# A 16-stage transformer kernel on one core: weight quantisation moved into the expert stages, loads, stores, a norm and the ends of four attention stages rearranged

## The chip, the core and the metric

The kernel runs on one NeuronCore of a Trainium2 chip. The metric is the device time of one execution in microseconds (us); lower is better. The core has five engines that each run their own instructions in order and wait for each other by semaphores: TensorE (PE in the profile, its weight loads PEld), VectorE (DVE), ScalarE (ACT), GpSimd (POOL) and SyncE (SP, which here only issues DMAs). A name with a q, such as SPq, is the engine's sequencer, which issues, waits or branches while the engine itself is idle.

## The reference

One activation `x` of 8 batches x 512 tokens x 128 channels, in fp32, goes through sixteen residual steps. Cut to what matters:

```python
x = X
x = x + attn0a(layernorm(x));  x = x + moe0(layernorm(x))     # 8 experts, top 2
x = x + attn0b(layernorm(x));  x = x + moe0(layernorm(x))
x = x + attn1a(layernorm(x));  x = x + moe1(layernorm(x))     # 8 experts, top 1
x = x + attn1b(layernorm(x));  x = x + moe1(layernorm(x))
x = x + attn2a(layernorm(x));  x = x + fp4_ffn2(layernorm(x)) # quantised weights
x = x + attn2b(layernorm(x));  x = x + fp4_ffn2(layernorm(x))
x = x + attn3a(layernorm(x));  x = x + fp4_ffn3(layernorm(x))
x = x + attn3b(layernorm(x));  x = x + fp4_ffn3(layernorm(x))

def fp4_quant_dequant(x):                # blocks of 16 along the last axis
    scale = max(max(|block|) / 6, 1e-12)
    return GRID[searchsorted(MID, |block / scale|)] * sign(block) * scale
def fp4_ffn(x, w_gate, w_up, w_down):    # 128 -> 352 -> 128
    q = fp4_quant_dequant
    h = silu(q(x) @ q(w_gate).T) * (q(x) @ q(w_up).T)
    return q(h) @ q(w_down).T
```

In `moe0` each token's two expert outputs are weighted by their gates, the token's normalised input is added, and the expert sum is itself layer-normalised. In `moe1` the output of the one chosen expert is added. `attn3b` is a mixer whose last part, the bus, adds to every token of a batch a vector that is computed from the batch's mean.

## The kernel before, in words

The activation `X` and its normalised form `XN` live in SBUF for the whole program, 32 tiles of 128 tokens (4 tiles to a batch). The program is a list of stages, each a `Block`: the engines' programs of a stage start together and the stage ends when the last engine is done. Names in the profile begin with the stage: `l0a`, `l0fa`, `l0b`, `l0fb`, `l1a`, `l1fa`, `l1b`, `l1fb`, `l2a`, `l2fa`, `l2b`, `l2fb`, `l3a`, `l3fa`, `l3b`, `l3fb`.

`load_stage` makes the constants on POOL, the largest and last of them `pick_rows` (L291, L295), and issues on SP one DMA for X and then one for each of 47 weights (L229, L233). Its block ends when SP has issued them all and X has landed. `norm_stage` normalises X on DVE and POOL by halves; it is used before `l0a` and before `l3fb`.

`routed_experts_stage` serves l0f (top 2) and l1f (top 1). It norms batch by batch, picks experts on DVE, sorts the tokens by expert with indirect DMAs on POOL (scatter into `rows_in`), runs fixed blocks of 128 rows, and gathers the results back on POOL (`back<-rows_out`). The batches are cut in chunks by `parts`, (2, 4, 2) in every expert stage; a chunk has `4*K*batches + 7` blocks, so 85 for l0f (K=2) and 53 for l1f (K=1). For a block DVE copies the expert's up weights (`fetch_up`, L3066), PE does the up product (L2817), ACT the Gelu (L2876, L2879) and PE the down product (L2832). While a chunk runs, POOL gathers the one before and scatters the one after, paced by the count of up products. `combine(b)` on DVE (L3037 to L3058) weights, normalises and adds what was gathered for a batch; in l0f ACT takes a square root for it in between (L2867), which DVE waits for and then refines by four small operations. `combine_at` says after which group of blocks a batch is combined. The batches of the last chunk, and those whose turn would come too late, are combined after all blocks.

`heads_attention_stage` serves l0b, l2a, l2b and l3a. A step T is one pair of heads: PE makes the transposed scores (L719) in the PSUM tile `ps_t`, ACT takes the exponential (L827), POOL masks it in the causal stages (L904), and PE multiplies with the values (L766) every second step. 3L steps ahead (L is 8 in l0b and 6 in the others) PE makes the scores once more in `ps_s`, for DVE to take the row maxima (L984). The next scores may only be written when the last exponential has been read out of `ps_t`:

```python
pe.wait_ge(probs_ready.sem, probs_ready.upto(T))
```

`quantized_weights_stage` (names `l2fa_w`, `l3fa_w`) runs before l2fa and before l3fa: DVE quantises `l2f_in` (88 partitions x 1024) and `l2f_out` (128 x 352) in ten operations each (L3150 to L3162), PE transposes them (L3206, L3209) and DVE copies them out of PSUM (L3196, L3198). `quantized_ffn_stage` reads the result. `bus_stage` ends `l3b`: three products (L2562 to L2567), then a scaling (L2578) and one addition over all of X (L2581). `store_stage` writes all of X with one DMA.

## Time and profile before

| what | value |
|---|---|
| median of 3 runs | 4066.81 us (4059.17 to 4073.92) |
| the profiled execution: time, span | 4060.57 us, 4058.8 us |
| TensorE clock granted, mean | 0.833 |
| busy: PE, DVE, ACT, POOL | 2890.8, 2672.3, 1814.9, 1708.3 us |
| load stage until the first instruction of the norm | 30.1 us |
| l0fa, l0fb | 291.5, 293.8 us |
| l1fa, l1fb | 206.1, 206.0 us |
| l0b, l2a, l2b, l3a | 513.4, 404.2, 411.9, 401.6 us |
| quantised weights: l2fa_w, l3fa_w | 16.7, 16.7 us |
| bus, norm before l3fb | 12.1, 23.5 us |

The span runs from the first to the last instruction; the execution's time has 1.8 us more. The stage times are from the first to the last instruction of the stage's names; between stages lie some 0.3 to 3 us. No engine is busy throughout, and the stages follow each other, so what an edit is worth has to be read in its own stage.

### The profile page before, as it was taken

What the parts mean: (1) busy time and instruction counts of PE and PEld (TensorE: products, weight loads), DVE (VectorE), ACT (ScalarE), POOL (GpSimd) and SP (SyncE); (2) the same over time, 40 slices, a digit from 0 to 9 for tenths busy, and PEclk for the clock granted to TensorE, in tenths of its full rate; (3) what the DMA queues carried; (4) which work ended last, traced back from release to release, by engine and by line L of the source; (5) the groups of instructions that cost most, each with busy time, mean ns of one, the idle gap of its engine ahead of it and who ended that gap; (6) DMA issues with size and microseconds to landing.
All of it is one profiled execution on the core that took longest, in us unless ns stands there. A gap on an engine that the chain in (4) does not pass through costs nothing. (4 is left out here: it accounts for less than half of the span.)

```text
span 4058.8 us, 65303 instructions
## 1 busy us (share of the span) xinstructions
PE 2890.8 (71%) x22525; PEld 1821.6 (45%) x22525; DVE 2672.3 (66%) x5940; ACT 1814.9 (45%) x3242; POOL 1708.3 (42%) x2364
## 2 busy tenths in 40 slices
PE   4868467775685759769588847688766888577846
PEld 3768312221684449558333325233344333254534
DVE  4644578884545853353588859688677888495767
ACT  2423247675322324434256634466543466444623
POOL 6743522220535113323456433355444455345753
PEclk9979679997687859869699968699877899786967
DMA  6122232210222012002222100222000221000000
GB/s 184 44 65 87 54 101 85 85 59 1 97 78 62 0 57 71 27 17 77 71 76 80 49 1 1 80 80 73 26 0 32 81 80 65 1 0 1 1 1 21
DMA packets 224583, 209.88 MB, mean 52 GB/s; under 512 B 49687, under 2 KB 201431, under 8 KB 223496
## 3 DMA queue, kind: packets, MB, share of 16 engines
q1 hardware_dynamic: 211976, 180.52, 13.8%
q0 software_dynamic: 12288, 25.19, 2.0%
q8 instruction: 190, 3.11, 0.3%
q14 instruction: 129, 1.06, 0.1%
HBM read 104.86 MB, written 98.83 MB: 50 GB/s over the span
## 5 line engine op out<-in xcount | busy, mean ns | idle before, releaser
L984 DVE TENSOR_REDUCE l0b_negm<-l0b_ps_s 128x2 f32<-128x1024 f32 x256 | 304.2, 1220 | 51.7 <-PE l0b_ps_s L737 50.6
L827 ACT ACTIVATE l0b_E<-l0b_ps_t 128x1024 f32<-128x1024 f32 x256 | 261.8, 1023 | 131.9 <-PE l0b_ps_t L719 131.8
L827 ACT ACTIVATE l2a_E<-l2a_ps_t 128x768 f32<-128x768 f32 (+1 forms) x192 | 169.2, 881 | 130.7 <-PE l2a_ps_t L719 129.9
L827 ACT ACTIVATE l3a_E<-l3a_ps_t 128x768 f32<-128x768 f32 (+1 forms) x192 | 169.2, 881 | 125.5 <-PE l3a_ps_t L719 124.6
L827 ACT ACTIVATE l2b_E<-l2b_ps_t 128x768 f32<-128x768 f32 (+1 forms) x192 | 169.1, 881 | 108.7 <-PE l2b_ps_t L719 107.7
L984 DVE TENSOR_REDUCE l2b_negm<-l2b_ps_s 128x2 f32<-128x256 f32 (+3 forms) x256 | 196.4, 818 | 28.8 <-PE l2b_ps_s L742 28.6
L984 DVE TENSOR_REDUCE l3a_negm<-l3a_ps_s 128x2 f32<-128x256 f32 (+3 forms) x256 | 196.4, 819 | 16.6 <-PE l3a_ps_s L742 16.5
L984 DVE TENSOR_REDUCE l2a_negm<-l2a_ps_s 128x2 f32<-128x256 f32 (+3 forms) x256 | 196.1, 817 | 15.3 <-PE l2a_ps_s L742 15.2
L904 POOL TENSOR_SCALAR_AFFINE_SELECT l2b_E<-l2b_E 128x256 f32<-128x256 f32 x256 | 100.3, 407 | 179.3 <-ACT l2b_E L827 179.3
L904 POOL TENSOR_SCALAR_AFFINE_SELECT l2a_E<-l2a_E 128x256 f32<-128x256 f32 x256 | 101.1, 407 | 167.5 <-ACT l2a_E L827 165.8
L904 POOL TENSOR_SCALAR_AFFINE_SELECT l3a_E<-l3a_E 128x256 f32<-128x256 f32 x256 | 101.1, 407 | 163.8 <-ACT l3a_E L827 162.2
L719 PE MATMUL l0b_ps_t<-room_up,room_down 51*128 51x512 bf16 x512 | 104.1, 403 | 82.7 <-ACT l0b_E L827 73.1
L766 PE MATMUL l0b_ps_v<-l0b_E,l0b_v 128*32 128x512 f32 x1024 | 144.9, 640 | 0.0
L719 PEld LDWEIGHTS l0b_ps_t<-room_up,room_down 51*128 51x128 bf16 x512 | 24.8, 93 | 229.6 <-ACT l0b_E L827 218.5
L2832 PE MATMUL l0fb_ps_y<-room_down,l0fb_hT 128*128 x680 | 97.8, 291 | 22.4 <-ACT l0fb_hT L2876 22.4
L2876 ACT ACTIVATE l0fb_hT<-l0fb_ps_u 128x512 f32<-128x512 f32 x85 | 50.3, 597 | 141.0 <-PE l0fb_ps_u L2817 141.0
L2876 ACT ACTIVATE l0fa_hT<-l0fa_ps_u 128x512 f32<-128x512 f32 x85 | 50.3, 597 | 138.5 <-PE l0fa_ps_u L2817 138.4
L2832 PE MATMUL l0fa_ps_y<-room_down,l0fa_hT 128*128 x680 | 96.1, 287 | 22.5 <-ACT l0fa_hT L2876 22.5
L737 PE MATMUL l0b_ps_s<-room_down,room_up 48*128 48x512 bf16 x512 | 86.8, 400 | 24.7 <-DVE l0b_negm L984 20.9
L719 PE MATMUL l2b_ps_t<-room_up,room_down 51*128 51x256 bf16 (+3 forms) x512 | 71.0, 316 | 44.2 <-ACT l2b_E L827 40.7
L2832 PEld LDWEIGHTS l0fb_ps_y<-room_down,l0fb_hT 128*128 128x128 f32 x680 | 90.2, 207 | 23.2 <-issue 23.2
L2817 PE MATMUL l0fb_ps_u<-l0fb_xT,l0fb_own_up 128*128 128x128 f32 x680 | 96.1, 288 | 4.7 <-DVE l0fb_xT L3020 4.7
(970 smaller groups left out, 8793.3 us busy)
## 6 DMA issues: line engine op xcount, KB each, us to landing
room_up<-l0b_stack SPq DMA_DIRECT2D x32, 192.0 KB
room_down<-l0b_stack SPq DMA_DIRECT2D x32, 192.0 KB
room_up<-l2a_stack SPq DMA_DIRECT2D x32, 192.0 KB
room_down<-l2a_stack SPq DMA_DIRECT2D x32, 192.0 KB
room_up<-l2b_stack SPq DMA_DIRECT2D x32, 192.0 KB
room_down<-l2b_stack SPq DMA_DIRECT2D x32, 192.0 KB
room_up<-l3a_stack SPq DMA_DIRECT2D x32, 192.0 KB
room_down<-l3a_stack SPq DMA_DIRECT2D x32, 192.0 KB
```

The costliest lines, as they stand in the source:

```text
L719: mm = pe.matmul(ps_t[:, hh, off:off + n], ks[b % 2][r, j, kt * P:(kt + 1) * P], qs[b % 2][r, j, first_q[kt]:S], start=True, stop=True)
L737: mm = pe.matmul(ps[:, hh, off:off + keys[qt]], qs[b % 2][r, j, qt * P:(qt + 1) * P], ks[b % 2][r, j, 0:keys[qt]], start=True, stop=not ca ...
L766: mm = pe.matmul(ps_v[32 * a:32 * a + 32, first_q[kt]:S], v_row[b % 2][:, kt, col:col + 32], e[:, a, off:off + w_k], start=(kt == 0), stop ...
L827: act.activation(probs(n % 3, c, 0)[:, 2 * p:2 * p + 2, :], ps_t[:, :, 0:width[c]], ACT.Exp, scale=scale).then_inc(probs_ready.sem, 1)
L904: kept = pool.affine_select(out=here, in_=here, compare_op=ALU.is_ge, fill=0.0, base=0, pattern=[[0, 2], [1, P]], channel_multiplier=-1)
L984: e = dve.tensor_reduce(negm[:, qt, :, j], ps_s[n % 2][:, :, off:off + keys[qt]], AX.X, ALU.max, negate=True)
L2817: mm = pe.matmul(ps_u[j % 4][:, c, :], own_up[j % 3][:, c * P:(c + 1) * P], xT[G % 2][:, k, :], start=True, stop=True)
L2832: mm = pe.matmul(ps_y[G % 2][:, k, :], hT[j % 3][:, c, :], down[:, bass.ds(e, 1), c, :].rearrange("p a b -> p (a b)"), start=(b2 is None a ...
L2876: a = act.activation(hT[j % 3][:, :, :], ps_u[j % 4][:, :, :], ACT.Gelu)
```

## The change

- **Loads.** `load_stage` issues X, `l0a_w` and `l0a_masks` only, and waits for these three. The other 45 weights are issued by SP inside the first `norm_stage`; SP waits for them at the end of the `l0a` stage. `pick_rows` is made by POOL at the end of that norm stage.
- **Stores.** `store_stage` is gone. SP stores each batch inside the last feed-forward stage.
- **Bus.** The scaling, the addition and the norm before l3fb are one loop over batches in the bus stage: DVE scales and adds, takes the statistics and shifts, POOL the roots, ACT normalises. The norm stage is gone.
- **Quantised weights.** The two stages are gone. The twenty DVE operations stand one by one in the block loop of l1fa (for layer 2) and l1fb (for layer 3), at blocks 8 to 27; PE transposes after the last block, DVE copies the result over the weights' own tiles.
- **Expert stages.** A batch is combined in steps: weighting at block START, statistics at START+1, rescaling and adding at START+3. The root is a `pow` on POOL; the four refining operations and ACT's square root are gone. POOL takes the roots of the late batches after its last gather. l1f has parts (4, 4) in place of (2, 4, 2): 46 blocks; l0f keeps (2, 4, 2).
- **Attention ends.** From step ALL-3L+2 on, when `ps_s` is no longer needed, the transposed scores go round `ps_t`, `ps_s[0]`, `ps_s[1]`, and PE waits for the exponential of three steps before.

```diff
+FIRST = ("l0a_w", "l0a_masks")
+def load_weight(core, sp, name):
+    src = core.dram[name]
+    return sp.dma_start(core.w[name][tuple(slice(0, x) for x in src.shape)], src)
...
-            for name, src in dram_now.items():
-                if name != "X":
-                    dst = core.w[name][tuple(slice(0, x) for x in src.shape)]
-                    sp.dma_start(dst, src).then_inc(core.loads, 16)
-            sp.wait_ge(done, 16)
+            for name in FIRST:
+                load_weight(core, sp, name).then_inc(done, 16)
+            sp.wait_ge(done, 16 * (1 + len(FIRST)))
...
         if core.loads_pending:
             @block.sync
             def _(sp):
-                sp.wait_ge(core.loads, pending)
+                for weight in core.dram:
+                    if weight != "X" and weight not in FIRST and weight not in LATER:
+                        load_weight(core, sp, weight).then_inc(core.loads, 16)
...
-                pe.wait_ge(probs_ready.sem, probs_ready.upto(T))
+                if T <= LAST:
+                    pe.wait_ge(probs_ready.sem, probs_ready.upto(T))
+                elif T <= LAST + 2:
+                    pe.wait_ge(scores_read.sem, scores_read.upto(ALL))
+                else:
+                    pe.wait_ge(probs_ready.sem, probs_ready.upto(T - 2))
...
-                        mm = pe.matmul(ps_t[:, hh, off:off + n], ks[b % 2][r, j, kt * P:(kt + 1) * P],
+                        mm = pe.matmul(scores_room(T)[:, hh, off:off + n], ks[b % 2][r, j, kt * P:(kt + 1) * P],
...
-            dve.tensor_scalar(y[:, :, :], ps_y[:, :, :], 0.1, None, ALU.mult).then_inc(copied, 1)
+            for b in range(B + 1):
+                if b < B:
+                    xb = core.X[:, b * TB:(b + 1) * TB, :]
+                    ch.link(dve.scalar_tensor_tensor(xb, ps_y[:, b, :].rearrange("p (a d) -> p a d", a=1).broadcast_to([P, TB, D]), 0.1, xb,
+                                                     ALU.mult, ALU.add))
+                    rows.statistics(dve, ch, b)
+                if b >= 1:
+                    rows.shifts(dve, b - 1)
...
+            def combine_roots(b):
+                pool.wait_ge(stats_ready.sem, stats_ready.upto(b + 1))
+                pool.tensor_tensor(rstd[:, b % 2, :], var[:, b % 2, :], core.minus_half[:, 0:TB], ALU.pow).then_inc(roots_ready.sem, 1)
...
             for t, k in moves(CHUNKS - 1):
                 gather_row(t, k)
+            for b in range(B):
+                if top2 and START[b] == LAST:
+                    combine_roots(b)
...
+            for j in range(LAST):
+                G = group_of[j]
+                if j == begin[G] and G + 1 < ALL:
                     read_xT(G + 1)
+                if j + 3 < LAST:
+                    fetch_up(j + 3)
+                if j + 1 == end[G]:
+                    read_y(G)
+                    if top2 and G < B:
+                        add_normed(G)
+                for b in range(B):
+                    if START[b] < LAST and 0 <= j - START[b] <= FINISH:
+                        combine_step(b, j - START[b])
+                if coming is not None and QUANTISE <= j < QUANTISE + 20:
+                    quantise_step(j - QUANTISE)
+            if coming is not None:
+                read_coming()
+            late = [b for b in range(B) if START[b] == LAST]
+            for b in late:
+                weigh(b)
+                if top2:
+                    moments(b)
+                    if b - 1 in late:
+                        add_scaled(b - 1)
+            if top2:
+                add_scaled(late[-1])
...
-    routed_experts_stage(core, name, w["l1f_gate"], w["l1f_bias"], w["l1f_up"], w["l1f_down"], b1=w["l1f_b1"], b2=w["l1f_b2"], parts=(2, 4, 2))
+    routed_experts_stage(core, name, w["l1f_gate"], w["l1f_bias"], w["l1f_up"], w["l1f_down"], b1=w["l1f_b1"], b2=w["l1f_b2"], parts=(4, 4),
+                         coming="l2f" if first else "l3f")
...
+                for b in range(B):
+                    sp.wait_ge(out_read.sem, out_read.upto(2 * (b + 1)))
+                    tiles = slice(b * TB, (b + 1) * TB)
+                    sp.dma_start(token_view(out)[:, tiles, :], core.X[:, tiles, :]).then_inc(stored, 16)
```

START of a batch is computed from the pace of the gathers. For l0f it is block 36, 44, 72 and 77 for batches 0 to 3, and batches 4 to 7 are late; for l1f it is 32, 36 and 40 for batches 0 to 2, and batches 3 to 7 are late.

## Rows read from the trace of the kernel before

**Rows 1.** The page, busy time of the engines in the whole span.

```profile
PE 2890.8 (71%) x22525; PEld 1821.6 (45%) x22525; DVE 2672.3 (66%) x5940; ACT 1814.9 (45%) x3242; POOL 1708.3 (42%) x2364
```

**Rows 2.** The DMAs of 0 to 12 us: issue, size, us to landing.

```profile
X<-in_X SPq DMA_DIRECT2D x1, 0.5 KB, 10.1
```

**Rows 3.** Timelines of 0 to 60 us: start, duration, engine, line, what.

```profile
9.44 3.38 POOL L295 TENSOR_SCALAR_AFFINE_SELECT pick_rows<-pick_rows 32x1024 bf16<-32x1024 bf16 x3
...
29.15 0.43 SPq L233 DMA_DIRECT2D l3b_bus<-in_l3b_bus  x1
...
30.08 0.87 DVE L348 BATCH_NORM_STATS2 l0a_norm_stats<-X 128x6 f32<-128x128 f32 x4 [30.08 <-PEq L226]
...
52.05 1.64 POOL L337 TENSOR_SCALAR XN<-X,l0a_norm_mv,l0a_norm_rstd 128x128 f32<-128x128 f32 x2
55.34 8.61 SPq L1551 DMA_DIRECT2D rows_in<-zeros  x2
```

**Rows 4.** The DMAs of 4040 to 4060 us and of 1630 to 1660 us.

```profile
out<-X SPq DMA_DIRECT2D x1, 2048.0 KB, 8.7
...
rows_out<-l1fa_y SPq DMA_DIRECT2D x2, 256.0 KB, 2.3
```

**Rows 5.** Timeline of the bus and the norm behind it.

```profile
3869.73 1.22 DVE L2578 TENSOR_SCALAR l3b_bus_y<-l3b_bus_ps_y 128x1024 f32<-128x1024 f32 x1 [3.66 <-PE l3b_bus_ps_y L2567]
...
3899.53 0.69 DVE L3305 TENSOR_REDUCE l3fb_x_scale<-XN 128x32 f32<-128x512 f32 x1 [1.41 <-PEq L313]
```

**Rows 6.** Timeline of the second weight stage and the start of l3fa.

```profile
3506.25 1.22 DVE L3150 TENSOR_REDUCE l3fa_w_scale<-l3f_in 88x64 f32<-88x1024 f32 x1 [2.00 <-PEq L497]
...
3509.79 0.69 DVE L3158 TENSOR_SCALAR l3fa_w_power<-l3fa_w_v 88x1024 uint32<-88x1024 uint32 x1
...
3523.28 0.69 DVE L3305 TENSOR_REDUCE l3fa_x_scale<-XN 128x32 f32<-128x512 f32 x1 [0.30 <-PEq L3170]
```

**Rows 7.** Instructions by line, l0fa, 300 to 450 us: busy, mean ns, idle before.

```profile
L2832 PE MATMUL l0fa_ps_y<-room_down,l0fa_hT 128*128 x504 | 72.0, 289 | 22.5 <-ACT l0fa_hT L2876 22.5
```

**Rows 8.** Timeline of the end of l0fa.

```profile
454.36 0.94 POOL L2733 DMA_INDIRECT l0fa_back<-rows_out,l0fa_slot_u  x1 [9.02 <-DMA rows_out<-l0fa_y]
...
473.62 0.94 POOL L2733 DMA_INDIRECT l0fa_back<-rows_out,l0fa_slot_u  x1 [0.30 <-issue]
476.08 0.88 DVE L3037 TENSOR_SCALAR l0fa_back<-l0fa_back,l0fa_gate 128x128 f32<-128x128 f32 x4 [3.86 <-DMA l0fa_back<-rows_out,l0fa_slot_u]
...
479.48 0.17 DVE L3049 TENSOR_SCALAR l0fa_var<-l0fa_mv 128x4 f32<-128x4 f32 x1
...
480.73 1.12 DVE L3056 TENSOR_SCALAR l0fa_back<-l0fa_back,l0fa_mv,l0fa_rstd 128x128 f32<-128x128 f32 x4
481.88 0.69 DVE L3058 TENSOR_TENSOR X<-X,l0fa_back 128x512 f32<-128x512 f32 x1
```

**Rows 9.** Timelines of l1fa: the first scatter, the third and the last Gelu.

```profile
1486.47 1.09 POOL L2729 DMA_INDIRECT rows_in<-XN,l1fa_slot_u  x1 [0.18 <-issue]
...
1524.80 1.14 ACT L2879 ACTIVATE l1fa_hT<-l1fa_ps_u,l1fa_b_block 128x128 f32<-128x128 f32 x4 [4.25 <-PE l1fa_ps_u L2817]
...
1649.46 1.14 ACT L2879 ACTIVATE l1fa_hT<-l1fa_ps_u,l1fa_b_block 128x128 f32<-128x128 f32 x4 [1.25 <-PE l1fa_ps_u L2817]
```

**Rows 10.** Busy time by engine in a stretch of l1fa's blocks.

```profile
1560.00:1600.00 40.00, 40.00 (x305) 36.14 (x305) 13.68 (x26) 18.18 (x65) 15.89 (x16) 1.00 0.26 77
```

**Rows 11.** Instructions by line, last 22 steps of l0b, 944 to 987.5 us.

```profile
L827 ACT ACTIVATE l0b_E<-l0b_ps_t 128x1024 f32<-128x1024 f32 x22 | 22.5, 1023 | 18.1 <-PE l0b_ps_t L719 18.1
L766 PE MATMUL l0b_ps_v<-l0b_E,l0b_v 128*32 128x512 f32 x88 | 18.7, 937 | 0.0
```

**Rows 12.** Busy time and granted clock in a stretch of these steps.

```profile
960.00:970.00 10.00, 7.76 (x34) 1.78 (x38) 1.21 (x5) 4.20 (x5) 1.26 (x1) 0.50 0.00 0
```

**Rows 13.** Instructions by line, last 14 steps of l2a, and of l3a.

```profile
L827 ACT ACTIVATE l2a_E<-l2a_ps_t 128x768 f32<-128x768 f32 (+1 forms) x14 | 12.2, 870 | 9.7 <-PE l2a_ps_t L719 9.7
...
L827 ACT ACTIVATE l3a_E<-l3a_ps_t 128x768 f32<-128x768 f32 (+1 forms) x14 | 12.2, 871 | 7.9 <-PE l3a_ps_t L719 7.7
```

More of the change, by code:

```diff
@@ L368, in _ @@
                 normalise(pool, b, (2, 3)).then_inc(pool_norm_ready.sem, 1)
+            if core.loads_pending:
+                pick = core.pick_rows
+                pool.memset(pick[:, :, :], 0.0).then_inc(core.picks_made, 1)
+                pool.wait_ge(core.picks_made, 1)
+                for k in range(3):
+                    r = slice(32 * k, 32 * k + 32)
+                    pool.affine_select(out=pick[r, :, :], in_=pick[r, :, :], compare_op=ALU.not_equal, fill=1.0, base=0,
+                                       pattern=[[-1, B], [0, P]], channel_multiplier=1).then_inc(core.picks_made, 1)
+                pool.wait_ge(core.picks_made, 4)
         if turned:
@@ L2577, in _, with routed_experts_stage @@
             dve.wait_ge(in_psum, 3)
-            dve.tensor_scalar(y[:, :, :], ps_y[:, :, :], 0.1, None, ALU.mult).then_inc(copied, 1)
-            dve.wait_ge(copied, 3)
-            x = core.X[:, :, :].rearrange("p (b t) d -> p b t d", b=B)
-            dve.tensor_tensor(x, x, y[:, :, :].rearrange("p b (a d) -> p b a d", a=1).broadcast_to([P, B, TB, D]),
-                              ALU.add).then_inc(copied, 1)
-def routed_experts_stage(core, name, w, bias, up, down, top2=False, b1=None, b2=None, parts=(4, 4)):
+            ch = Chain(dve_step, dve, 0)
+            for b in range(B + 1):
[6 more added lines that the diff above has]
+                    rows.shifts(dve, b - 1)
+            dve_step.per = ch.k
+        @block.gpsimd
+        def _(pool):
+            for b in range(B):
+                rows.roots(pool, b)
+        @block.scalar
+        def _(act):
+            for b in range(B):
+                rows.normalise(act, b)
+    core.end(1, [dve_step])
+    for unused in (rows.T_in_psum, rows.T_ready):
+        unused.per = 0
+    rows.end()
+def routed_experts_stage(core, name, w, bias, up, down, top2=False, b1=None, b2=None, parts=(4, 4), coming=None):
     nc = core.nc
@@ L2863, in _ @@
                 expert_exponentials(1)
-            def roots(b):
-                act.wait_ge(stats_ready.sem, stats_ready.upto(b + 1))
-                act.activation(rstd[:, :], var[:, :], ACT.Sqrt).then_inc(roots_ready.sem, 1)
             for j in range(LAST):
@@ L2881, in _ @@
                 a.then_inc(act_ready.sem, 1)
-                if top2 and j + 1 == end[group_of[j]]:
-                    for b in combine_at(group_of[j]):
-                        roots(b)
-            if top2:
-                for b in combine_at(ALL):
-                    roots(b)
         @block.vector
@@ L3092, in routed_experts_stage @@
     stats_ready.per = roots_ready.per = B * top2
+    quant_ready.per = quantT_in_psum.per = int(coming is not None)
     core.end(1, sig)
@@ L3260, in blocks, with _ @@
             return x.rearrange("p t (n c) -> p (t n) c", c=BLOCK)
+        if out is not None:
+            stored = core.ctx.enter_context(nc.semaphore("stored"))
+            @block.sync
+            def _(sp):
+                for b in range(B):
+                    sp.wait_ge(out_read.sem, out_read.upto(2 * (b + 1)))
+                    tiles = slice(b * TB, (b + 1) * TB)
+                    sp.dma_start(token_view(out)[:, tiles, :], core.X[:, tiles, :]).then_inc(stored, 16)
+                sp.wait_ge(stored, 16 * B)
         def x_tiles(u):
@@ L3494, in attention_program @@
             stage(core)
-        store_stage(core, out)
 def layer0_attention_a(core):
```

273 lines of the change are left out of this document (134 added, 139 removed).

## The prediction

> **What bounds the kernel now.** I read the page first. No engine is near full: PE is busy for 71% of the span, DVE for 66% [rows 1], and the chain that ended last reaches back only into the last feed-forward stage. The stages run one after another, so I looked up where each begins and ends, and then, at the places that the diff touches, the timelines, the instructions by line and the windows. What the reader is to see is a set of stretches in which most engines wait for one thing: SP's issues at the start, DVE alone on the weights, POOL's gathers behind the expert blocks, one PSUM tile at the ends of the attentions. The change goes at eight such stretches, and the sum is theirs. It is made against the profiled execution (4060.6 us, its span and 1.8 us around it), which lies 6.2 us under the median of 4066.8; the saving is then taken from the median.
>
> **Loads: minus 16.** The norm starts at 30.08, when SP has issued its last weight at 29.15 to 29.58 [rows 3], though X had landed 10.1 us after its issue at 0.85, at 11.0 [rows 2]. Behind X only two small loads are left, so the norm should start at about 11 (10 to 12): 19 saved. Given back: POOL makes `pick_rows` behind its last normalisation, which ends at 53.7; the three selects take 3.38 and the memset about 1, so the stage, which gave way at 55.3, ends some 3 us later relative to its start [rows 3]. SP's 45 issues at 0.47 us (one of many such in a row; the last is in [rows 3]) take 21 to 22 us and stay under the stage's 28. If they took as long as the whole load stage, 28 us, they would still be level with POOL. The wait for them at the end of l0a, a whole stage on, costs nothing. 16, between 14 and 18.
>
> **Stores: minus 7.** The output's one DMA lands 8.7 us after its issue; 256 KB to HBM land in 2.3 [rows 4]. Seven of eight batches leave during the stage. 6.5, and with the missing stage border 7.
>
> **Bus and norm: minus 9.** From the end of the products to the first instruction of l3fb pass 3899.53 - 3869.73 = 29.8 us [rows 5]. The joint loop costs DVE per batch one scaled add over 512 columns (0.69, as the addition of that size in [rows 8]), statistics, aggregation, variance (1.4 together, four tiles at the 0.87 of [rows 3] and the small ones) and a shift, about 2.15; eight make 17.2. Behind the last come a root (1.0), the shift, ACT's four tiles (1.7) and the border: 3.4. 29.8 - 20.6 = 9, between 7 and 10.
>
> **The two weight stages: minus 34.** The second takes 3523.28 - 3506.25 = 17.0 with its border, the first the same [rows 6]. The work goes into l1f's blocks. Its largest operation is 1.22 us, five of 20 are; the 20 sum to 13. DVE is busy 13.7 of 40 us there and PE 40 of 40 at full clock [rows 10], and the copies of up weights have two blocks of lead, so I cost it at nothing: PE's work is the cover. Without that cover it would cost 13 per stage. The final transposes and copies, about 4, lie in the wait for the last stores and gathers.
> One rule speaks against this. The rows show 0.69 us for each of two big `tensor_scalar` operations on SBUF [rows 6]. The Trainium skill, "SBUF — State Buffer", section "SBUF: two separate sides", says that while DVE is in a two-port mode GpSimd can't write the descriptors of its DMAs. By that rule the four such operations of a stage would hold back POOL's scatters by at most 2 us in all; by the rows POOL is busy 15.9 of 40 us and idle in front of each paced DMA [rows 10], which takes it up. Either way the sum stays.
>
> **l1f in two chunks: minus 13 for both.** The third to the last Gelu of 53 take 1649.46 - 1524.80 = 124.7 for 50 blocks, 2.49 each [rows 9]; seven blocks fewer save 17.5. The last chunk has four batches, so 8 more gathers at 1.25 us (the pace of [rows 8]) stand behind the last store: 10 given back. In front, the first route waits for four batches, and 16 rather than 8 tiles are scattered before the first fetch: the first scatter moves from 1486.5 to about 1490, and 16 at 1.26 end near 1510, with landing, fetch and transpose 1516. Before, DVE's routing of the other chunks let the first product start only near 1515, so only 1 to 2 are lost. Net 6 to 7 per stage, 13 for both (between 6 and 18).
>
> **l0f: minus 34 for both.** Between 300 and 450 us PE is idle for 22.5 us in front of the down product, waiting for a Gelu [rows 7]: ACT stands in the square root of a combine, behind DVE, four times in the stage. Some 5 us more go in products at half clock after these waits. Spread over four blocks, with the root on POOL, this goes, except where POOL, which in the last chunk issues DMAs without a gap, comes late with batches 2 and 3: I give back 3. So the blocks end about 24 us earlier. At the end the change is dearer. Today DVE combines as the data come and is done at 482.57, 8.0 us after the last gather's end at 474.56 [rows 8]. After, the root of batch 4 stands behind all 16 gathers, and everything that follows on DVE waits for it: root 1.1; then in order rescale(4) 1.8, weigh and statistics(6) 3.6, rescale(5) 1.8, weigh and statistics(7) 3.6, rescale(6) 1.8, rescale(7) 1.8. The 3.6 is 476.08 to 479.65, the 1.8 is 480.73 to 482.57 [rows 8]. That makes 15.6 in place of 8.0: 7.5 given back. 24 - 7 = 17 per stage, 34 for both, between 16 and 42.
>
> **Attention ends: minus 27.** In l0b's last 22 steps ACT's exponentials take 22.5 us and wait 18.1 us for PE's scores [rows 11], because PE may write them only after the exponential before. With three tiles PE runs ahead. If it is at full clock, nearly all of the 18 goes, 16. It is at the lower level of 1.2 GHz there now and busy 78% [rows 12]: if that stays, the 43.5 us hold 34 us of PE work, and 9.5 go. The value products are the dearest, 937 ns for one of four that overlap [rows 11]. Full clock is likelier, since less waiting leaves PE busier; I take 12. In the last 14 steps of l2a the waits are 9.7, in l3a 7.9, and l2b is as l3a [rows 13]; a read of the group's output and POOL's masks leave 3 to 4 of them: 6 + 4.5 + 4.5 = 15. Together 27, between 17 and 38.
>
> **Sum.** 16 + 7 + 9 + 34 + 13 + 34 + 27 = 140. The profiled execution would be near 3921, the median 4066.8 - 140 = 3927; the three runs of before lie between 4059 and 4074, so I round to 3925.
>
> **Rivals.** (a) The l0f tail eats more and PE stays at 1.2 GHz at the attention ends: l0f 8 per stage, ends 17 together, 140 - 18 - 10 = 112 saved, 3955. For it: the clock of [rows 12]. Against: that clock is seen while PE waits.
> (b) The added DVE steps are not hidden in l1f: 2 x 13 for the operations and 2 x 4 for the transposes and copies, 140 - 34 = 106, 3961. Against it: [rows 10].
> (c) All goes by the better bounds: loads 18, stores 7, bus 10, weights 34, l1f 16, l0f 42, ends 38: 165, 3902. For it: PE is idle only where it waits for what is removed.
> (d) Slower than before. The DVE steps thin PE's stream in l1f so far that the lower clock level is granted for the blocks. PE is full there at the higher level [rows 10], so a block would cost up to 2.4 more, and the 92 blocks of both stages 220: 4147. It decides once 58 of the 92 blocks run at the low level. Against it: PE has two blocks of lead over DVE.
>
> **How the numbers follow.** Chances: my sum 0.70, (a) 0.12, (b) 0.05, (c) 0.11, (d) 0.02. 3925 is the likeliest case. The range 3895 to 3968 takes in (a), (b) and (c) with the scatter of the runs (some 7 us either way) and leaves out (d) and the far ends of the parts. A change within 0.3% (12 us) is what a measurement of this kernel can't tell from none; all cases but (d) are far past it, so faster 0.97, same 0.01, slower 0.02.
>
> **What would show it.** The norm starting at about 11 us and l0a at about 39; no names of weight stages or of the last norm; the first operation of l3fb some 21 us after the bus products; a last DMA of 2 to 3 us. In l0fa no Sqrt on ACT and next to no idle PE in front of the down products, but the last DVE instruction 15 to 16 us behind the last gather. In l1fa 46 blocks still 2.5 apart, with DVE near half busy, and the last gather 20 us after the first of its batch. In l0b's last 22 steps exponentials 1.05 to 1.5 us apart. The prediction would be wrong if blocks 8 to 27 of l1f are longer than the others, if POOL's roots hold DVE in the middle of l0f, or if the granted clock of the attention ends stays 0.5 and their steps as long as now.

## The result, and the profile after

| what | before | after |
|---|---|---|
| median of 4 runs each | 4066.1 us (4059.2 to 4073.9) | 3919.3 us (3917.5 to 3924.9) |
| ratio, 95% interval | | 0.9641 (0.9621 to 0.9661) |
| the profiled execution: time, span | 4060.6, 4058.8 us | 3924.9, 3923.1 us |
| TensorE clock granted, mean | 0.833 | 0.842 |

The change saves 146.8 us by the medians and 135.7 us by the two profiled executions; 140 was predicted, and 3925 for the median, 3921 for the profiled execution. The first line of the page, the answer to [rows 1]:

```profile
PE 2817.3 (72%) x22261; PEld 1768.3 (45%) x22261; DVE 2638.8 (67%) x5824; ACT 1783.6 (45%) x3184; POOL 1713.8 (44%) x2364
```

Where the 135.7 us came from, as stage to stage distances (first instruction of a stage to the first of the next) of the two traces:

| term | predicted | measured | what it is made of |
|---|---|---|---|
| loads | 16 | 14.1 | norm starts 17.4 earlier, its stage is 3.3 longer |
| stores | 7 | 7.9 | l3fb with the store 159.3 to 151.4 |
| bus and norm | 9 | 8.6 | 36.2 to 27.6 |
| two weight stages | 34 | 34.1 | 17.0 each |
| l1f in two chunks, with the quantise steps | 13 | 15.2 | 7.5 and 7.7 |
| l0f | 34 | 25.1 | 11.8 and 13.3 |
| attention ends | 27 | 30.7 | l0b 17.5, l2a 5.2, l2b 3.1, l3a 4.9 |
| the rest | 0 | 0.0 | l3fa 1.9 shorter, mixer 3.0 longer, and others |

**The start.** DMAs of 0 to 14 us (issue, size, us to landing), the answer to [rows 2]:

```profile
l0a_masks<-in_l0a_masks SPq DMA_DIRECT2D x1, 66.5 KB, 4.9
...
X<-in_X SPq DMA_DIRECT2D x1, 0.5 KB, 10.0
```

and the timeline of 0 to 43 us, the answer to [rows 3]:

```profile
0.85 0.91 SPq L238 DMA_DIRECT2D X<-in_X  x1
...
1.81 5.48 SPq L173 DMA_DIRECT2D l0a_w<-in_l0a_w  x1
...
7.33 0.43 SPq L173 DMA_DIRECT2D l0a_masks<-in_l0a_masks  x1
...
12.68 0.87 DVE L338 BATCH_NORM_STATS2 l0a_norm_stats<-X 128x6 f32<-128x128 f32 x4 [12.68 <-PEq L235]
...
36.27 0.95 POOL L361 MEMSET pick_rows<- 96x1024 bf16 x1
37.37 3.38 POOL L365 TENSOR_SCALAR_AFFINE_SELECT pick_rows<-pick_rows 32x1024 bf16<-32x1024 bf16 x3
41.21 1.89 POOL L1612 MEMSET l0a_v<- 128x2144 f32 x1 [0.46 <-POOLq L303]
```

X lands at 10.9, but the norm starts at 12.7: SP is held for 5.5 us by its second issue, so `l0a_masks` is issued only at 7.3 and lands at 12.2. The 45 later loads don't show: `pick_rows` closes the stage. The kernel before has the same hold at its second issue, of another weight, and its trace could have told of it:

```profile
1.80 5.40 SPq L233 DMA_DIRECT2D rope<-in_rope  x1
```

**Stores and bus.** The last output DMAs (answer to [rows 4]), and the timeline from the end of the bus products to l3fb (answer to [rows 5]):

```profile
out<-X SPq DMA_DIRECT2D x3, 256.0 KB, 2.3
```

```profile
3750.66 0.69 DVE L2594 SCALAR_TENSOR_TENSOR X<-l3b_bus_ps_y,X 128x512 f32<-128x512 f32 x1 [3.84 <-PE l3b_bus_ps_y L2579]
...
3771.71 0.69 DVE L3372 TENSOR_REDUCE l3fb_x_scale<-XN 128x32 f32<-128x512 f32 x1 [2.31 <-PEq L2557]
```

21.05 us in place of 29.8.

**l1fa.** A stretch of the blocks that carry the quantise steps, 40 us with busy time by engine (PE, PEld, DVE, ACT, POOL), granted clock, DMA share and GB/s; the answer to [rows 10]:

```profile
1500.00:1540.00 40.00, 40.00 (x305) 36.14 (x305) 20.23 (x40) 18.34 (x66) 8.90 (x10) 1.00 0.24 67
```

DVE has 6.5 us more to do than in [rows 10], PE is still busy throughout and at full clock.

**l0fa.** Its down products between 280 and 412 us (instructions by line), the answer to [rows 7]; the idle time in front of them is gone:

```profile
L2887 PE MATMUL l0fa_ps_y<-room_down,l0fa_hT 128*128 x512 | 69.0, 279 | 0.0
```

The end of the stage, the answer to [rows 8]:

```profile
419.28 0.17 DVE L3155 TENSOR_SCALAR l0fa_var<-l0fa_mv 128x4 f32<-128x4 f32 x1
...
434.12 0.94 POOL L2774 DMA_INDIRECT l0fa_back<-rows_out,l0fa_slot_u  x1 [0.30 <-issue]
435.08 2.02 POOL L2779 TENSOR_TENSOR l0fa_rstd<-l0fa_var,minus_half 128x4 f32<-128x4 f32 x2
...
436.16 1.11 DVE L3161 TENSOR_SCALAR l0fa_back<-l0fa_back,l0fa_mv,l0fa_rstd 128x128 f32<-128x128 f32 x4 [16.71 <-POOL l0fa_rstd L2779]
...
447.04 1.03 POOL L2779 TENSOR_TENSOR l0fa_rstd<-l0fa_var,minus_half 128x4 f32<-128x4 f32 x1 [4.32 <-DVE l0fa_var L3155]
...
449.89 0.69 DVE L3164 TENSOR_TENSOR X<-X,l0fa_back 128x512 f32<-128x512 f32 x1
...
457.60 0.88 DVE L413 BATCH_NORM_STATS2 l0b_row_stats<-X 128x6 f32<-128x128 f32 x4 [7.01 <-PEq L2639]
```

DVE has the variances of batches 4 and 5 at 419.4 and then waits 16.7 us for their roots, which stand behind the gathers; that was foreseen. The last line was not: DVE is done at 450.6, but the next stage starts 7.0 us later. Before, it started 1.5 us after DVE. The engine that closes the stage is POOL. Its sequencer has a record there that the timeline leaves out (start, us):

```
447.01 10.31 POOL sequencer L2639 DRAIN
457.36  0.02 POOL sequencer L2639 EVENT_SEMAPHORE
```

Each stage ends with one on each engine. On POOL most of them end at most 0.3 us after POOL's last instruction; those of the expert stages end 9.2 us after it in l0f and 5.3 us after it in l1f, before the change as after it.

**Attention ends.** Instructions by line in the last 22 steps of l0b, the answer to [rows 11]:

```profile
L836 ACT ACTIVATE l0b_E<-l0b_ps_s 128x1024 f32<-128x1024 f32 x14 | 14.0, 1048 | 1.9 <-PE l0b_ps_s L728 1.9
L775 PE MATMUL l0b_ps_v<-l0b_E,l0b_v 128*32 128x512 f32 x92 | 13.2, 644 | 3.7 <-ACT l0b_E L836 2.1 <-ACT l0b_oT L844 1.6
L836 ACT ACTIVATE l0b_E<-l0b_ps_t 128x1024 f32<-128x1024 f32 x8 | 8.4, 1046 | 0.3 <-PE l0b_ps_t L728 0.3
```

and busy time by engine in two stretches of them, the answer to [rows 12]:

```profile
925.00:935.00 10.00, 8.57 (x66) 1.80 (x64) 2.93 (x13) 9.67 (x11) 0.76 (x1) 1.00 0.00 1
935.00:945.00 10.00, 8.00 (x60) 1.69 (x60) 0.55 (x2) 9.67 (x12) 0.51 (x1) 1.00 0.00 0
```

ACT waits 2.2 us instead of 18.1, and the granted clock in these stretches is 1.00 instead of 0.50 (over the 22 steps 0.93 instead of 0.62). The 22 steps take 24.4 us instead of 43.9. In the last 14 steps of l2a and l3a, the answer to [rows 13], ACT still waits 4.0 and 4.8 us:

```profile
L836 ACT ACTIVATE l2a_E<-l2a_ps_s 128x768 f32<-128x768 f32 (+1 forms) x9 | 8.0, 905 | 4.0 <-PE l2a_ps_s L728 4.0
...
L836 ACT ACTIVATE l3a_E<-l3a_ps_s 128x768 f32<-128x768 f32 (+1 forms) x9 | 8.1, 908 | 4.8 <-PE l3a_ps_s L728 4.8
```

### The profile page after: what moved, and what is told of

Same layout as the page of the kernel before. It is cut to its first block and busy times, and to the rows that moved or that the text cites. A ratio compares the mean times of both kernels' runs of the same rounds, so it can differ in the third digit from the quotient of the medians.

```text
span 3923.1 us, 64375 instructions
## 1 busy us (share of the span) xinstructions
PE 2817.3 (72%) x22261; PEld 1768.3 (45%) x22261; DVE 2638.8 (67%) x5824; ACT 1783.6 (45%) x3184; POOL 1713.8 (44%) x2364
## 3 DMA queue, kind: packets, MB, share of 16 engines
q1 hardware_dynamic: 208376, 178.69, 14.1%
## 5 line engine op out<-in xcount | busy, mean ns | idle before, releaser
L836 ACT ACTIVATE l0b_E<-l0b_ps_t 128x1024 f32<-128x1024 f32 x242 | 247.8, 1024 | 117.6 <-PE l0b_ps_t L728 117.4
L836 ACT ACTIVATE l2a_E<-l2a_ps_t 128x768 f32<-128x768 f32 (+1 forms) x182 | 160.4, 881 | 119.7 <-PE l2a_ps_t L728 118.9
L836 ACT ACTIVATE l3a_E<-l3a_ps_t 128x768 f32<-128x768 f32 (+1 forms) x182 | 160.4, 881 | 117.1 <-PE l3a_ps_t L728 116.3
L993 DVE TENSOR_REDUCE l2a_negm<-l2a_ps_s 128x2 f32<-128x256 f32 (+3 forms) x256 | 195.9, 816 | 14.9 <-PE l2a_ps_s L751 14.8
L836 ACT ACTIVATE l2b_E<-l2b_ps_t 128x768 f32<-128x768 f32 (+1 forms) x182 | 160.3, 881 | 100.3 <-PE l2b_ps_t L728 99.5
L728 PE MATMUL l0b_ps_t<-room_up,room_down 51*128 51x512 bf16 x484 | 96.2, 394 | 70.2 <-ACT l0b_E L836 60.9
L728 PEld LDWEIGHTS l0b_ps_t<-room_up,room_down 51*128 51x128 bf16 x484 | 23.3, 93 | 204.5 <-ACT l0b_E L836 193.8
L746 PE MATMUL l0b_ps_s<-room_down,room_up 48*128 48x512 bf16 x512 | 87.8, 404 | 25.7 <-DVE l0b_negm L993 22.7
L2872 PE MATMUL l0fa_ps_u<-l0fa_xT,l0fa_own_up 128*128 128x128 f32 x680 | 94.1, 283 | 9.3 <-DVE l0fa_xT L3120 4.8
L775 PE MATMUL l2b_ps_v<-l2b_E,l2b_v 128*32 128x512 f32 (+3 forms) x1024 | 93.9, 463 | 8.9 <-POOL l2b_E L913 6.9
L775 PE MATMUL l2a_ps_v<-l2a_E,l2a_v 128*32 128x512 f32 (+3 forms) x1024 | 91.7, 453 | 4.9 <-ACT l2a_oT L844 2.3
L775 PE MATMUL l3a_ps_v<-l3a_E,l3a_v 128*32 128x512 f32 (+3 forms) x1024 | 91.6, 452 | 4.7 <-ACT l3a_oT L844 2.9
## 6 DMA issues: line engine op xcount, KB each, us to landing
room_up<-l0b_stack SPq DMA_DIRECT2D x32, 192.0 KB
room_down<-l0b_stack SPq DMA_DIRECT2D x32, 192.0 KB
room_up<-l2a_stack SPq DMA_DIRECT2D x32, 192.0 KB
room_down<-l2a_stack SPq DMA_DIRECT2D x32, 192.0 KB
room_up<-l2b_stack SPq DMA_DIRECT2D x32, 192.0 KB
room_down<-l2b_stack SPq DMA_DIRECT2D x32, 192.0 KB
room_up<-l3a_stack SPq DMA_DIRECT2D x32, 192.0 KB
room_down<-l3a_stack SPq DMA_DIRECT2D x32, 192.0 KB
```

The lines of the kernel that those rows point to most:

```text
L728: mm = pe.matmul(scores_room(T)[:, hh, off:off + n], ks[b % 2][r, j, kt * P:(kt + 1) * P], qs[b % 2][r, j, first_q[kt]:S], start=True, sto ...
L746: mm = pe.matmul(ps[:, hh, off:off + keys[qt]], qs[b % 2][r, j, qt * P:(qt + 1) * P], ks[b % 2][r, j, 0:keys[qt]], start=True, stop=not ca ...
L775: mm = pe.matmul(ps_v[32 * a:32 * a + 32, first_q[kt]:S], v_row[b % 2][:, kt, col:col + 32], e[:, a, off:off + w_k], start=(kt == 0), stop ...
L836: act.activation(probs(n % 3, c, 0)[:, 2 * p:2 * p + 2, :], scores_room(T)[:, :, 0:width[c]], ACT.Exp, scale=scale).then_inc(probs_ready.s ...
L993: e = dve.tensor_reduce(negm[:, qt, :, j], ps_s[n % 2][:, :, off:off + keys[qt]], AX.X, ALU.max, negate=True)
L2872: mm = pe.matmul(ps_u[j % 4][:, c, :], own_up[j % 3][:, c * P:(c + 1) * P], xT[G % 2][:, k, :], start=True, stop=True)
```

## The experiments

All start from the kernel after. Total times are medians of four runs; the kernel after was 3919.3. An untouched stage can differ by 2 to 7 us from one run to the next (below), so effects of a few us are read in their own stage.

### The late roots on ACT

POOL's part behind its last gather goes, ACT's comes behind its last Gelu; the third hunk is `add_scaled` on DVE.

```diff
-            for b in range(B):
-                if top2 and START[b] == LAST:
-                    combine_roots(b)
...
+            for b in range(B):
+                if top2 and START[b] == LAST:
+                    act.wait_ge(stats_ready.sem, stats_ready.upto(b + 1))
+                    act.activation(rstd[:, b % 2, :], var[:, b % 2, :], ACT.Sqrt).then_inc(roots_ready.sem, 1)
...
+                if START[b] == LAST:
+                    r, v = rstd[:, u, :], var[:, u, :]
+                    ch.link(dve.reciprocal(r, r))
+                    ch.link(dve.scalar_tensor_tensor(corr[:, :], r, -0.5, r, ALU.mult, ALU.mult))
+                    ch.link(dve.tensor_tensor(corr[:, :], corr[:, :], v, ALU.mult))
+                    ch.link(dve.scalar_tensor_tensor(r, corr[:, :], 1.5, r, ALU.add, ALU.mult))
```

> Base: the kernel after. In l0fa and l0fb the four roots of the batches that are combined after all blocks (4 to 7) go from POOL to ACT (a Sqrt, then a reciprocal and three small DVE operations); POOL keeps the roots inside the loop. In the kernel after, POOL's last gather of l0fa ends at 435.1 us, its last root at 448.1, DVE's last addition at 450.6, and the next stage's first instruction starts at 457.6, 7.0 after it, when POOL's sequencer record DRAIN has ended. Theory A (the stage's end is POOL's closing DRAIN, and that ends some 9.3 us after POOL's last instruction, whatever it is): POOL's last instruction is now the last gather, so the border lies at 435.1 + 9.3 = 444.4 or at the end of DVE's additions, whichever is later; DVE no longer waits 16.7 us for roots behind the gathers and ends near 444. 12 to 13 us shorter per stage, 25 in all. Rival B (the border follows DVE's end by 7 us for another reason): DVE's end moves by 6 to 7 us and the border with it, 13 us in all. Rival C (the DRAIN lasts from the last gather, and roots behind it cost nothing): the next stage starts at the same time as now, 0 us in all.

Measured: 3890.0 us, ratio to the kernel before 0.9567 (0.9551 to 0.9583); l0fa 11.0 and l0fb 11.7 us shorter. Timeline of the end of l0fa:

```profile
434.70 0.95 POOL L2775 DMA_INDIRECT l0fa_back<-rows_out,l0fa_slot_u  x1 [0.30 <-issue]
...
445.42 0.69 DVE L3172 TENSOR_TENSOR X<-X,l0fa_back 128x512 f32<-128x512 f32 x1
446.65 0.87 DVE L413 BATCH_NORM_STATS2 l0b_row_stats<-X 128x6 f32<-128x128 f32 x4 [0.54 <-PEq L2639]
```

POOL's DRAIN ends at 444.9, 9.2 us after the last gather, and DVE at 446.1 is last again: the border is 0.5 us. 22.7 us of the 29 stand in these two stages; B asked for 13 and C for none. Theory A holds, less 1 to 2 us because DVE ends 2 us later than I had worked out.

### An explicit drain ahead of the last gathers

```diff
+            pool.drain()
             wait_stored(CHUNKS - 1)
             for t, k in moves(CHUNKS - 1):
                 gather_row(t, k)
```

> Base: the kernel after, with one explicit drain on POOL in each expert stage, ahead of the gathers of the last chunk (112 of l0f's 128 indirect DMAs and 48 of l1f's 64 are then issued). The closing DRAIN ends 9.3 us after POOL's last instruction in l0f and 5.3 us in l1f: 1.3 us plus 0.0625 us for each indirect DMA of the stage fits both. Theory A (the drain pays for each indirect DMA since the drain before): the added drain takes 8.3 us in l0f, where POOL has only 4.5 us to spare (last gathers start 3.8 later), and the closing one 2.3 instead of 9.3, so the stage is about 3 us shorter; in l1f POOL is idle for 22 us there, so the added drain is hidden and the next stage starts 2 to 3 us earlier (DVE's last addition is then last). About 10 us less in all. Rival B (the closing DRAIN is a fixed time after the last DMAs, or is set by the stage): the closing one stays at 9.3 and 5.3 us, l0f gets up to 5 us longer per stage and l1f stays: 0 to 10 us more in all.

Measured: 3904.3 us; l1fa and l1fb 2.7 and 2.5 us shorter, l0fa 0.5 longer, l0fb 2.3 shorter. Timeline of POOL and DVE around the two drains of l0fa and behind the last gather of l1fa:

```profile
411.40 0.94 POOL L2774 DMA_INDIRECT l0fa_back<-rows_out,l0fa_slot_u  x1 [0.30 <-issue]
422.33 0.94 POOL L2774 DMA_INDIRECT l0fa_back<-rows_out,l0fa_slot_u  x1 [9.99 <-issue]
...
456.82 0.69 DVE L3165 TENSOR_TENSOR X<-X,l0fa_back 128x512 f32<-128x512 f32 x1
458.05 0.87 DVE L413 BATCH_NORM_STATS2 l0b_row_stats<-X 128x6 f32<-128x128 f32 x4 [0.54 <-PEq L2639]
...
1595.21 0.87 DVE L413 BATCH_NORM_STATS2 l1b_row_stats<-X 128x6 f32<-128x128 f32 x4 [0.53 <-PEq L2639]
```

The added drain takes 9.2 us in l0fa (412.3 to 421.6, with 112 indirect DMAs issued) and 4.0 in l1fa (48), where it lies in idle time. The closing one ends 1.4 us after POOL's last instruction in l0fa and 2.2 after it in l1fa, at 1592.4 to 1594.6 (16 DMAs each), instead of 9.2 and 5.3. So a drain pays for what was issued since the drain before it, and it can be paid early. Rival B is out. 4.0, 5.3 and 9.2 us for 48, 64 and 112 are 0.08 us each, and 128 take 9.2 as well; my line of 1.3 + 0.0625 gave 8.3 for 112 and was 0.9 too low. The 3 us that theory A expected of an l0f stage did not come in l0fa: POOL's last root ends 7.0 us later there, and DVE, done at 457.5, is last. Why l0fb gained 2.3 all the same is not shown. The stages give 7.1 us together, the medians 15.0 and the two profiled executions 22.0; of the difference in the latter 11.8 us lie in stages that the edit doesn't touch (l0b 5.5, l2a 3.3, mixer 3.0).

### l1f in three chunks again

```diff
-    routed_experts_stage(core, name, w["l1f_gate"], w["l1f_bias"], w["l1f_up"], w["l1f_down"], b1=w["l1f_b1"], b2=w["l1f_b2"], parts=(4, 4),
+    routed_experts_stage(core, name, w["l1f_gate"], w["l1f_bias"], w["l1f_up"], w["l1f_down"], b1=w["l1f_b1"], b2=w["l1f_b2"], parts=(2, 4, 2),
```

> Base: the kernel after, with l1f's experts in three chunks (2, 4, 2) again, 53 blocks instead of 46 in l1fa and in l1fb. The step of the prediction was 13 us for both stages (6 to 18); the stages themselves became 7.5 and 7.7 us shorter. If the two chunks did all of that: 13 to 16 us slower, each l1f stage by 6.5 to 8. Rival (the chunks are worth their blocks in full, at 2.39 us for a block of l1fa and 7 blocks fewer, and the quantise steps took some of it back): 30 us slower, or more.

Measured: 3927.1 us. l1fa is 5.2 and l1fb 8.2 us longer, 13.4 together, as in the prediction's step. The medians show 7.8 of it and the two profiled executions 2.8: in the latter l0b was 7.0 and l2b 3.7 us shorter, with the same code. The rival is out, and its block was wrong: from the third to the last Gelu the blocks of l1fa are 2.49 us apart in both kernels and in this run, not 2.39. Seven of them are 17.5 us, and the last gather ends 23.1 us behind the last down product with two chunks and 13.4 with three, so the prediction's 10 given back are there too and nothing is left to explain. That l1fa lost less than l1fb lies ahead of the blocks: its third Gelu comes 60.5 us into the stage in this run, that of l1fb after 62.3.

### One PSUM tile for the last scores

```diff
-            return (ps_t, ps_s[0], ps_s[1])[(T - LAST) % 3] if T >= LAST else ps_t
+            return ps_t
...
-                if T <= LAST:
-                    pe.wait_ge(probs_ready.sem, probs_ready.upto(T))
-                elif T <= LAST + 2:
-                    pe.wait_ge(scores_read.sem, scores_read.upto(ALL))
-                else:
-                    pe.wait_ge(probs_ready.sem, probs_ready.upto(T - 2))
+                pe.wait_ge(probs_ready.sem, probs_ready.upto(T))
```

> Base: the kernel after, with the last scores of l0b, l2a, l2b and l3a again all in one PSUM tile and each behind the exponential before it. The stages became 17.5, 5.2, 3.2 and 4.9 us shorter. If that is all due to the three tiles: 31 us slower, more than half of it in l0b, with the last exponentials of l0b again 1.5 to 2.4 us apart (they are 0.90 to 0.92 apart now). Rival (part of it came from the stages ahead of them or from the clock): under 25 us slower.

Measured: 3966.5 us, 47 more. Instructions by line in l0b's last 22 steps:

```profile
L831 ACT ACTIVATE l0b_E<-l0b_ps_t 128x1024 f32<-128x1024 f32 x22 | 22.5, 1024 | 19.2 <-PE l0b_ps_t L723 19.2
L770 PE MATMUL l0b_ps_v<-l0b_E,l0b_v 128*32 128x512 f32 x88 | 19.5, 977 | 0.0
```

and all 22 steps by engine (PE first, then PEld, DVE, ACT, POOL), in this run and in the kernel after:

```profile
916.90:961.90 45.00, 32.29 (x146) 6.28 (x146) 3.84 (x16) 24.02 (x26) 1.26 (x1) 0.59 0.00 1
920.80:945.20 24.40, 20.77 (x146) 4.83 (x145) 3.85 (x16) 22.15 (x26) 1.27 (x1) 0.93 0.01 2
```

From the first of the last 22 exponentials (l0b) or 14 (the others) to the end of the last: 45.0, 25.0, 23.6 and 24.0 us with one tile; 24.4, 16.8, 16.0 and 17.5 with three. The difference is 20.6 + 8.2 + 7.6 + 6.5 = 42.9 us, more than either theory. Of l0b's 20.6, ACT's waits are 19.2 - 2.2 = 17, and 2.7 (22 times 0.12) is that exponentials of 1.02 us follow each other every 0.90 us once their input is ready. Seen from TensorE, its idle time falls by 9.1 us (12.7 to 3.6) and the same 146 products take 11.5 us less, at a mean clock of 0.93 instead of 0.59; no run changes the clock alone. The rival falls too: ahead of the ends the four stages differ by at most 1 us each.

The edit does not give back the times of before, though the code of these steps is the same: before they took 43.9, 23.9, 21.4 and 21.4 us, 7.0 less in all, at mean clocks of 0.62, 0.64, 0.84 and 0.84, and here they run at 0.59, 0.56, 0.71 and 0.64. So the change itself brought 35.9 us in these steps, and the other 7.0 of the 42.9 go with the clock that this run happened to get in them.

### No quantise steps in l1f

The twenty operations of each l1f stage are left out, so the weights of layers 2 and 3 are transposed but not quantised.

```diff
-                if coming is not None and QUANTISE <= j < QUANTISE + 20:
-                    quantise_step(j - QUANTISE)
+                if coming is not None and j == QUANTISE + 19:
+                    dve.sem_inc(quant_ready.sem, 1)
```

> Base: the kernel after without the twenty quantise operations in each l1f stage; the weights of layers 2 and 3 are transposed but left unquantised. Theory (they are hidden behind blocks that TensorE bounds at full clock): l1fa and l1fb stay within 1 us each of 201.9 and 201.6 us. Rival (b of the prediction, they sit in DVE's way to the next block): up to 13 us less in each, 26 in all. The 7 blocks fewer should have brought 16.7 us per stage at 2.39 us each and brought 7.6; if the quantise operations took the rest, 9 us less in each.

Measured: 3915.4 us (3911.6 to 3923.7), which overlaps the runs of the kernel after. l1fa takes 201.8 us as before the edit (201.9), l1fb 204.5 instead of 201.6, longer with less work: its clock reached 1.00 in the fifth stretch of 20 us instead of the fourth. The stretch of l1fa's blocks by engine:

```profile
1494.00:1534.00 40.00, 40.00 (x306) 36.14 (x305) 11.95 (x24) 18.34 (x66) 8.78 (x10) 1.00 0.24 67
```

DVE loses 8.3 of its 20.2 us and PE runs on as it did. The steps are hidden in full; rival (b) is out. The transposes and copies, which this run keeps, lie in the 23.1 us between the last down product and the last gather: DVE's last addition of l1fa ends 2.3 us behind the last gather, before the change and after it.

### pick_rows in the load stage

The first hunk is POOL's program in the load stage, the second the one in `norm_stage`.

```diff
+            pool.memset(pick[:, :, :], 0.0).then_inc(core.picks_made, 1)
+            pool.wait_ge(core.picks_made, 1)
+            for k in range(3):
+                r = slice(32 * k, 32 * k + 32)
+                pool.affine_select(out=pick[r, :, :], in_=pick[r, :, :], compare_op=ALU.not_equal, fill=1.0, base=0,
+                                   pattern=[[-1, B], [0, P]], channel_multiplier=1).then_inc(core.picks_made, 1)
             pool.wait_ge(made, 33)
+            pool.wait_ge(core.picks_made, 4)
...
-            if core.loads_pending:
-                pick = core.pick_rows
-                pool.memset(pick[:, :, :], 0.0).then_inc(core.picks_made, 1)
...
-                pool.wait_ge(core.picks_made, 4)
```

> Base: the kernel after, with the memset and the three selects of pick_rows again at the end of POOL's work in the load stage. There the stage already waits until 12.2 us for the last of its three transfers, and POOL's part (5.5 us for these four, from the 36.3 to 40.8 us that they take now and a memset) would end near 13. Theory: the norm starts about 0.5 us later and the norm's stage is 3.2 us shorter (28.5 to 25.3), 2.5 to 3 us less in all. Rival: POOL's work in the load stage ends later than that and the load stage gives all of it back: 0.

Measured: 3911.2 us. Timeline:

```profile
9.43 3.38 POOL L302 TENSOR_SCALAR_AFFINE_SELECT pick_rows<-pick_rows 32x1024 bf16<-32x1024 bf16 x3
...
13.37 0.87 DVE L346 BATCH_NORM_STATS2 l0a_norm_stats<-X 128x6 f32<-128x128 f32 x4 [13.37 <-PEq L235]
```

The norm starts 0.7 us later, its stage is 3.3 us shorter, and l0a starts at 38.6 instead of 41.2: 2.6 us, as expected. The other 5 us of the total are not the edit's.

### All roots on ACT

On top of the late roots on ACT; the lines stand behind the Gelu of block j, and the four refining operations now follow every root. POOL takes none: its list `rooted_within` is empty.

```diff
+                for b in range(B):
+                    if top2 and START[b] < LAST and j == START[b] + FINISH - 1:
+                        act.wait_ge(stats_ready.sem, stats_ready.upto(b + 1))
+                        act.activation(rstd[:, b % 2, :], var[:, b % 2, :], ACT.Sqrt).then_inc(roots_ready.sem, 1)
```

> Base: the kernel roots_on_act; now the four roots inside the block loop are ACT's too, each behind the Gelu of the block in which POOL took it, with a reciprocal and three small DVE operations behind it. The split of a batch's combining over four blocks stays. Compared are l0fa and l0fb (270.2 and 270.1 us in roots_on_act). Theory A (the loop's gain of 24.5 us per stage came from ACT no longer waiting between two Gelus for a root's input, and from no change of ACT's function tables): with the input ready two blocks before, only the changes of table are left, twice 1 to 1.3 us for each of four roots, 5 to 10 us more per stage. Rival B (it was the split over four blocks alone): the stages stay within 2 us. Rival C (ACT's queue is the bound, any root in it stalls the Gelu for good): 20 to 25 us more per stage, as before.

Measured: 3905.0 us; l0fa 280.0 and l0fb 279.9 us, 9.8 more each than with the loop's roots on POOL. ACT, and the down products, between 300 and 407 us, by line:

```profile
L2941 ACT ACT_TABLE_LOAD x4 | 5.1, 1283 | 0.1
L2932 ACT ACT_TABLE_LOAD x3 | 3.8, 1283 | 0.1
L2941 ACT ACTIVATE l0fa_rstd<-l0fa_var 128x4 f32<-128x4 f32 x3 | 0.6, 205 | 5.4 <-DVE l0fa_var L3161 5.4
...
L2885 PE MATMUL l0fa_ps_y<-room_down,l0fa_hT 128*128 x400 | 54.0, 279 | 6.7 <-ACT l0fa_hT L2932 6.7
```

Timeline of ACT around one of these roots:

```profile
335.88 1.28 ACT L2941 ACT_TABLE_LOAD   x1
339.10 0.21 ACT L2941 ACTIVATE l0fa_rstd<-l0fa_var 128x4 f32<-128x4 f32 x1 [1.93 <-DVE l0fa_var L3161]
339.32 1.28 ACT L2932 ACT_TABLE_LOAD   x1
340.61 1.09 ACT L2932 ACTIVATE l0fa_hT<-l0fa_ps_u 128x512 f32<-128x512 f32 x2
```

The size is that of theory A, at its upper end: 9.8 / 4 = 2.45 us for each root in the loop. Its reason holds in part. The two table loads of 1.28 us are there, but the input is not ready: ACT waits another 1.6 to 2.5 us for the variances at each of the four roots (5.0 at each before the change). A root holds ACT for 4.4 to 5.3 us between two Gelus, and how the 2.45 us that reach the blocks divide between loads and wait is not shown. B and C are out. The Trainium skill, "ScalarE: Activation LUTs", section "What ACT_TABLE_LOAD costs", gives 1.28 us for the load and 2.66 for a whole switch. The load agrees with this trace, the whole switch does not: from the end of the Sqrt to the start of the next Gelu pass 1.30 us (339.31 to 340.61). An estimate from the page's larger figure, two switches for each of four roots, would be 21 us of ACT. The blocks end 245.2 us into the stage here, 260.0 before the change and 235.4 after it. So 14.8 of the 24.5 us came from splitting the combining over four blocks and 9.8 from taking the root away from ACT, with its loads, the wait that was left and the refining operations.

### Combined

The late roots on ACT, `pick_rows` in the load stage, and the explicit drain in l1f alone.

```diff
+            if not top2:
+                pool.drain()
             wait_stored(CHUNKS - 1)
```

> Base: the kernel roots_on_act (3890.0 us), with pick_rows made in the load stage and with POOL's explicit drain ahead of the last gathers in the l1f stages alone, where POOL is idle for 22 us. Theory: 3 us less from the first, 2.5 to 2.8 us less in each of the two l1f stages as in drain_early, so 8 to 8.5 less: 3881 to 3882 us. Rival (the gains don't add, the clock takes them back): 3885 us or more.

Measured: 3881.0 us (3875.9 to 3883.7), ratio to the kernel before 0.9555 (0.9539 to 0.9571). The l1f stages are 2.9 us shorter each, l0a starts 2.6 us earlier, l0f as with the roots on ACT. The gains add up.

### Combined, with one more drain and another order at l0f's end

```diff
+                if top2 and c == 1:
+                    pool.drain()
                 wait_stored(c - 1)
...
             for b in late:
+                awaited = b >= first_batch[CHUNKS - 1]
+                if top2 and awaited:
+                    add_scaled(b - 1)
                 weigh(b)
                 if top2:
                     moments(b)
-                    if b - 1 in late:
+                    if not awaited and b - 1 in late:
                         add_scaled(b - 1)
```

> Base: the kernel combined (3881.0 us), where DVE's last addition of l0fa ends at 441.2 us and the next stage starts at 441.8. Two edits in l0f: one more explicit drain on POOL, ahead of its wait for the first chunk's stored rows, where POOL is idle for 15 us in l0fa; and on DVE the scaling and addition of the batch before goes ahead of the wait for the gathers of batches 6 and 7 instead of behind their moments. Theory (the closing DRAIN pays for what was issued since the last drain, now 80 indirect DMAs instead of 128, some 6.5 us instead of 9.2 after the last gather; DVE has one scaling and addition less, 1.7 to 2.7 us, behind the last gather): the next stage starts 1.5 to 2.5 us earlier, 3 to 5 us less in all, 3876 to 3878 us. Rival (the closing DRAIN does not get shorter by a drain that far back): it ends 9.2 us after the last gather, which is 1.3 us before the start of the next stage now, so at most 1.3 us less per stage.

Measured: 3880.3 us (3878.9 to 3887.6), ratio 0.9538 (0.9519 to 0.9557); l0fa 1.6 and l0fb 2.1 us shorter. Timeline of the end of l0fa:

```profile
430.71 0.94 POOL L2774 DMA_INDIRECT l0fa_back<-rows_out,l0fa_slot_u  x1 [0.30 <-issue]
...
439.08 0.69 DVE L3175 TENSOR_TENSOR X<-X,l0fa_back 128x512 f32<-128x512 f32 x1
440.31 0.87 DVE L412 BATCH_NORM_STATS2 l0b_row_stats<-X 128x6 f32<-128x128 f32 x4 [0.54 <-PEq L2638]
```

The closing DRAIN ends at 438.2, 6.6 us after the last gather, for 80 DMAs: 6.5 was expected. The stages show the 3.7 us; the total can't be told from the kernel combined, because l2fa, l2fb, l2b and the mixer took 1.6 to 2.9 us more each.

## Why the prediction was right

The total was right (3919 against 3925, inside the range) because the mechanisms and most of the terms were. That it came so close is in part luck: against 140 the two profiled executions give 135.7, in which l0f is 8.9 and the loads 1.9 short, and the attention ends 3.7 and l1f 2.2 over; and the medians differ by 11 us more than the profiled executions.

- **Loads, 14.1 for 16.** The step "behind X only two small loads are left, so the norm should start at about 11" failed by 0.7 us against its own upper bound of 12: the issue of the second load held SP for 5.5 us, and l0a starts at 41.2 instead of about 39. The 3 us for `pick_rows` were right, and `picks_in_load` gets 2.6 back.
- **Stores 7.9, bus 8.6, weights 34.1** for 7, 9 and 34. The bus loop has a period of 2.19 us for 2.15. That the steps are covered is shown by `no_quantise`.
- **l1f, 15.2 for 13**, and 13.4 when undone alone. 17.5 saved and 10 given back were right to 0.1 us in l1fa. The 1 to 2 us in front were not lost: the third Gelu comes 63.1 us into the stage before and after. (The prediction's own terms, 17.5 - 10 - 1 to 2, make 5.5 to 6.5 per stage, not the 6 to 7 it wrote.)
- **l0f, 25.1 for 34.** The blocks end 24.5 us earlier (24 in the sum), and DVE ends 38.7 us behind them instead of 31.5, so 7.2 are given back (7.5 in the sum): 17.3 per stage up to there. DVE's last addition ends 15.5 us behind the last gather, as foreseen. What "24 - 7 = 17 per stage" lacked is the stage's end: I took DVE's last addition for it. It is POOL's DRAIN, which ends 9.2 us behind POOL's last instruction. Before, that instruction was the last gather and DVE's 8.0 us hid nearly all of it; after, it is a root 13.0 us later, and 5.5 us come out at the border of each stage. `roots_on_act`, `drain_early` and `combined2` show this from three sides. That l0fb gained 1.5 us more than l0fa was not followed up.
- **Attention ends, 30.7 for 27**, and 35.9 in the last steps alone (19.5, 7.1, 5.4, 3.9); l0b took some 4 us more ahead of its end than before the change and in most later runs. The step "if it is at full clock, nearly all of the 18 goes, 16 ... I take 12" was mis-sized: 19.5 us went. The clock was mostly at its upper level (0.93 over the steps, where it had been 0.62), and exponentials at 0.90 us, where 1.05 to 1.5 was foreseen, took away 2.7 us that I had counted as ACT's floor.

Rival (a) had the l0f tail right in kind and the clock wrong; (c) was nearer at the ends; (b) and (d) did not occur.

## What to carry to other kernels

When work moves to the engine that closes a stage, read what closes it: here a drain whose length follows the indirect DMAs of the stage and whose start follows the engine's last instruction, so roots of 1 us put last on POOL cost 5.5 us of border per stage on top of DVE's wait. Pay such a drain in idle time, and let another engine take what must come late. Where TensorE takes turns with another engine and its granted clock is low, removing the wait can bring more than the idle time in TensorE's row: 20.6 us in l0b's last steps, where that row had 12.7, with a mean clock of 0.59 before the wait was gone and 0.93 after.
